# Attention on one core: rounding the next pair's q and k behind the transposed blocks' copies of the same slot

## The reference, cut to what matters

```python
q = rope(xn @ q_w + q_b)            # 16 heads of 64
k = rope(xn @ k_w + k_b)
scores = (q @ k.T) / sqrt(64)
attn = softmax(where(causal, scores, -inf))
ctx = attn @ (xn @ v_w + v_b)
attn_out = ctx @ o_w + o_b + xn
```

## Time and profile before

| | |
|---|---|
| median of 3 runs | 2509.33 us (2506.49 to 2509.35) |
| profiled execution | 2507.55 us, of which the instructions span 2505.6 us |
| TensorE busy | 2063.1 us (82%), weight loads beside it 1363.4 us |
| VectorE busy | 1666.8 us (67%) |
| ACT busy | 1440.3 us (57%) |
| POOL busy | 920.0 us (37%) |
| mean granted TensorE clock | 0.916 |

### The profile page before, as it was taken

One profiled execution on the slowest core, in us unless ns is written; L12 is line 12 of the kernel. 1 busy time (PEld: TensorE's weight loads), 2 busy tenths in 40 slices (PEclk: granted clock), 3 DMA queues, 4 the chain that ended last, 5 costly groups with the idle time before them and its releaser, 6 DMA issues.

```text
span 2505.6 us, 41253 instructions
## 1 busy us (share of the span) xinstructions
PE 2063.1 (82%) x10326; PEld 1363.4 (54%) x10326; DVE 1666.8 (67%) x2947; ACT 1440.3 (57%) x2785; POOL 920.0 (37%) x797
## 2 busy tenths in 40 slices
PE   3749999879675999987966699996996669999698
PEld 1236666547324666655732466664662256666466
DVE  3957676669485666647948666674794766666488
ACT  2517676647542766655744366674674346766366
POOL 1544343223164434313315444341332453434222
PEclk9879999979796999997979799999897979999899
DMA  2000000001000000001100000000110000000011
GB/s 60 0 26 5 9 8 0 1 28 40 10 0 26 10 5 8 0 1 34 34 10 0 26 10 5 8 0 9 30 30 10 13 14 8 9 4 0 11 34 32
DMA packets 36210, 35.48 MB, mean 14 GB/s; under 512 B 3992, under 2 KB 30976, under 8 KB 36096
## 3 DMA queue, kind: packets, MB, share of 16 engines
q1 hardware_dynamic: 36096, 34.14, 4.7%
HBM read 32.03 MB, written 2.10 MB: 14 GB/s over the span
## 4 chain that ended last, share of the span: by engine, by line
PE 59%; DVE 20%; issue 10%; ACT 5%; POOL 4%; DVEq 1%; ACTq 0%; DMA 0%; POOLq 0%; SPq 0%
PE ps L1341 10%; PE ps L1180 7%; PE ps L1181 7%; PE ps L1182 7%; PE ps L1330 6%; DVE state L930 6%; PE ps L1320 4%; PE ps L1321 4%; PE ps L1356 3%; PE ps L1448 2%; PE ps L1208 2%; DVE q_split L993 2%; PE ps L1172 2%; DVE bx L923 2%; DVE ps L1008 1%
## 5 line engine op out<-in xcount | busy, mean ns | idle before, releaser
L707 ACT ACTIVATE probsT<-ps 128x512 f32<-128x512 f32 (+3 forms) x768 | 349.6, 493 | 382.4 <-PE ps L1330 381.7
L695 ACT ACTIVATE probs<-ps,least 128x640 f32<-128x640 f32 (+7 forms) x512 | 380.6, 743 | 65.4 <-DVE least L1003 59.5
L1330 PE MATMUL ps<-ident,probs 128*128 128x128 f32 x2304 | 349.4, 279 | 10.4 <-ACT probsT L707 10.2
L1320 PE MATMUL ps<-k_high,q_split 128*128 128x512 f32 (+3 forms) x768 | 309.2, 403 | 57.8 <-POOL k_low L550 38.6
L1330 PEld LDWEIGHTS ps<-ident,probs 128*128 128x128 f32 x2304 | 262.9, 141 | 128.2 <-issue 91.6
L538 POOL TENSOR_TENSOR roped<-turned 128x512 f32<-128x512 f32 x128 | 192.6, 1506 | 286.1 <-DVE turned L978 274.2
L1341 PE MATMUL ps<-probsT,vals 128*64 128x512 f32 (+3 forms) x1536 | 290.4, 502 | 5.2 <-ACT probsT L707 5.2
L1003 DVE CUSTOM_DVE_ANT_0 ps<-ps,row_masks 128x128 f32<-128x128 f32 (+3 forms) x256 | 127.6, 499 | 235.2 <-PE ps L1321 232.5
L1010 DVE TENSOR_REDUCE least<-ps 128x1 f32<-128x640 f32 (+3 forms) x256 | 262.3, 1025 | 9.1
L1321 PE MATMUL ps<-k_low,q_split 128*128 128x512 f32 (+3 forms) x768 | 259.0, 349 | 0.0
L755 ACT ACTIVATE hid<-ps,cols 128x512 f32<-128x512 f32 x256 | 176.4, 689 | 105.2 <-PE ps L1182 77.1
(11 more groups left out here) (213 smaller groups left out, 4252.2 us busy)
## 6 DMA issues: line engine op xcount, KB each, us to landing
w<-in_w SPq DMA_DIRECT2D x128, 128.0 KB, 2.0
w_pair<-in_w_pairs SPq DMA_DIRECT2D x36, 256.0 KB, 2.7
xin<-in_x SPq DMA_DIRECT2D x5, 512.0 KB, 3.9
out<-acc SPq DMA_DIRECT2D x4, 512.0 KB, 4.1
pos<-in_c_pos SPq DMA_DIRECT2D x1, 512.0 KB, 5.5
v_w<-in_v_w SPq DMA_DIRECT2D x1, 512.0 KB
o_w<-in_o_w SPq DMA_DIRECT2D x1, 512.0 KB
v_b<-in_v_b SPq DMA_DIRECT2D x1, 512.0 KB
```

Source lines behind the costliest of these rows:

```text
L695: act.activation(probs[:, t % 2, 0:width(t)], banks(2 * (t % 2))[:, 0:width(t)], ACT.Exp, bias=least[:, t:t + 1], scale=-1.0, accum_out=ro ...
L707: act.activation(dst, ps[:, T_BANK + g % 2, 0:k1 - k0], ACT.Copy).then_inc(t_taken, 1)
L1320: pe.matmul(o, q, k_high[par][h][:, k0:k1], start=True, stop=False)
L1330: made = pe.transpose(ps[:, T_BANK + g % 2, at - k0:at - k0 + P], probs[:, t % 2, at:at + P], ident[:, :])
```

## The change

In ACT's `step`, the rounding of a slot is issued behind the copies of the transposed block instead of ahead of them. It concerns slots 5, 6, 9 and 10 of the first seven pairs of each batch.

```diff
@@ -720,12 +720,12 @@
                             keep_factors(n - 1, 1, x_at(p, "old", 0, first, last))
                         if t == SPREAD_AT[0]:
                             keep_factors(n, 0, x_at(p, "own", 0, first, last))
-                        if t in HIGH_AT and not last:
-                            high(n + 1, 1 - par, *HIGH_AT[t])
                         if t > 0:
                             keep_turned(n, t - 1)
                         elif not first:
                             keep_turned(n - 1, UNITS_A - 1)
+                        if t in HIGH_AT and not last:
+                            high(n + 1, 1 - par, *HIGH_AT[t])
```

## The result

| | before | after |
|---|---|---|
| median | 2509.34 us (2506.49 to 2509.73, 4 runs) | 2535.23 us (2533.49 to 2538.1, 4 runs) |
| ratio to before | | 1.0106, 95% interval 1.009 to 1.0122 |
| span of the profiled execution | 2505.6 us | 2531.5 us |
| mean granted TensorE clock | 0.916 | 0.916 |

What follows compares the result with a forecast made beforehand. TensorE was busy 82% of the span, with VectorE's full queue leading slots 7 to 10. 24 x 0.95 = 22.8 plus 4 x 0.71 = 2.8 gave 25.6 us more: median 2535.0 us, range 2523 to 2543.

Steps and rivals of the forecast that it cites:

- Slot 5, 0.95 us in 24 pairs: Steady pairs: the moved rounding delays exponential 6 and the scores of unit 8 by 0.95 us, bracket nothing to 1.08.
- Slot 5, 0.71 in four first pairs: First pair of each batch, no ACT idle time in slot 5: exponential at 193.40 against 192.69, 0.71 us later.
- Slots 6, 9 and 10, nothing: Roundings moved in these three slots delay later exponentials, but TensorE wants those later still: cost nothing.
- cover of slot 9: Slot 9: exponential 10's reading ends at 281.98, TensorE wants it at 282.65: 0.67 us of cover.
- cover of slot 6: Slot 6: exponential 7 is ready at 275.32, scores of unit 9 want it at 276.21: 0.89 us of cover.
- Low parts and POOL, nothing: VectorE's low parts of q and POOL's of k wait for their own queues, not ACT's roundings: no cost.
- the booked wait in the first pairs: TensorE's scores of unit 8: booked wait for ACT around 0.6 us or more in 24 pairs, shorter in four first pairs.
- VectorE leads the pair there: Slots 7 to 10: VectorE's full queue, busy 7.77 of 8.00 us, leads the pair, so delayed unit 8 scores delay the rest.
- Rival A: Behind slot 6: an unseen slack swallows the 0.95 us, ACT being idle 43% of the span; 2509 us, chance 0.05.
- Rival B: TensorE's or VectorE's queue gives some back, leaving 0.3 to 0.6 us a pair; 2522 us, chance 0.08.
- Rival C: Slots 9 and 10 are exposed too, up to 0.95 us more a pair; 2562 us, chance 0.04.
- Rival D: Slots 6, 9 and 10: earlier copies free transpose banks, so transposes start sooner; 2499 us at best, chance 0.02.

Runs made afterwards that it cites:

- only_6_9_10: Kernel before with the roundings of slots 6, 9 and 10 put behind the copies, slot 5 in the old order: 2507.04 us, ratio 1.0002.
- low11_after: Kernel before with all four roundings behind the copies and VectorE's second low part of q in slot 11 instead of 8: 2507.65 us.
- double5_ahead: Kernel before with an idle second rounding added in slot 5, ahead of the copy: 2499.81 us.
- double9_ahead: Kernel before with an idle second rounding added in slot 9, both roundings ahead of the copies: 2508.01 us, ratio 0.9999.
- the two halves: Two kernels, each with part of the change against the kernel before: slot 5 alone, ratio 1.0108; slots 6, 9 and 10 alone, ratio 1.0002.
- double9_behind: Kernel before with slot 9's k rounding put behind the copies, together with an idle second rounding of the same size: 2497.62 us.
- low_at_11: Kernel before with VectorE's second low part of q moved from slot 8 to slot 11: 2473.84 us, ratio 0.9864.
- low_at_12: Kernel before with VectorE's second low part of q moved from slot 8 to slot 12: 2485.56 us.

## Why the prediction was right

*Slot 5, 0.95 us in 24 pairs.* Right in place, size and mechanism: the steady pairs went from 40.1 and 40.5 us (they alternate) to 41.0 and 41.5. The bracket of nothing to 1.08 was closed by the row of another rounding, and that row, not the middle of the bracket, was the measured value. *Slot 5, 0.71 in four first pairs:* 0.71 from exponential 5 to exponential 6 in each; up to slot 9 the four batches are 0.64, 0.76, 0.75 and 0.75 longer, 2.9 in all against 2.8. *Slots 6, 9 and 10, nothing:* shown by only_6_9_10, and the cover of slot 9 by spending it. The cover of slot 6 was put too high: 0.89 was worked out, and in the kernel after the scores of unit 9 start only 0.60 behind the reading of exponential 7, because TensorE comes to them 2.80 us after the scores of unit 8 and not 2.97. That cost nothing. *Low parts and POOL, nothing:* TensorE's wait for POOL's low parts of k is 38.7 us after and 38.6 before. The sum, 25.6, stands against 25.9 between the medians and 26.4 in the attention. The 24 steady pairs as measured are 22.5 us longer and the first pairs 2.9, together 25.4; the remaining us of the attention lies in the last pairs, which are 0.2 to 0.3 longer each, a term that the sum put at nothing and that I did not explain. One sign was wrong: the booked wait in the first pairs is 0.69 as in the steady ones, and not shorter.

One reason carried less than the prediction put on it. "VectorE leads the pair there" is true: in the kernel after, TensorE's wait for the values is 1.29 instead of 1.12, so VectorE's queue swallows the 0.17 that TensorE gains. But low11_after shows that the exchange costs 0.86 of the 0.95 once VectorE has slack. The rest of the delay is passed on by the second way, from TensorE through exponential 8 to the scores of unit 10, which the prediction did not name.

That the median fits to 0.3 us is in part luck. The time outside the attention has more than one value (below), up to 5 us a batch apart, and the prediction had no term for it; before and after happen to lie on the same side.

*Rival A.* ACT is busy 57% of the time and has idle time in every pair, but the moved rounding has left an idle stretch for one place that has none. The advice of the Trainium skill (Perfetto Trace Analysis, Identifying the Most-Contended Engine), to improve the engine of the highest occupancy, does not tell the price of an order on a less busy one: 25.9 us here. double5_ahead and double9_ahead are the other side of this: a whole added rounding a pair, at the right place, costs a steady pair nothing. *Rival B* and *Rival C* fell with the two halves, *Rival D* with the unchanged 10.2 us of the earlier trace rows.

## What to carry to other kernels

An instruction on an engine with idle time is free only inside a particular stretch of it; ask of each idle stretch who ends it and what is queued behind, and count a moved instruction at its start-to-start time if it lands between a release and the instruction that someone waits for. A start that always follows its release by the same small latency (0.05 to 0.06 us here) is a critical hand-over even where no wait is booked. In a steady pair of the kernel before six of the sixteen units release TensorE so (units 2, 4, 6, 8, 13 and 15, in all 24 pairs), and only that of unit 6 has an edited slot just ahead of it; what a delay costs at the other five was not tried. Two ways can also be tight at one place, and slack on one of them then gives little back. Compare stages by their own time before reading a small difference of medians as the effect of an edit: in double9_behind the direct cost and a gain elsewhere have opposite signs.

## What was not expected

Several kernels with *more* work or later work in the attention ran faster than before or than foreseen, because the time outside the attention, which no edit touched, has more than one value: 305.3 us a gap, or 299.9 to 300.6. The gap after the first batch, busy time by stretch (columns as in the earlier trace rows), in before, in low_at_11 and in double9_behind:

```profile
493.70:798.90 305.20, 224.35 (x838) 134.53 (x836) 206.02 (x308) 149.92 (x214) 112.14 (x106) 0.84 0.07 21
```

```profile
488.00:788.10 300.10, 218.55 (x838) 130.02 (x836) 205.99 (x308) 149.66 (x214) 112.15 (x106) 0.87 0.07 22
```

```profile
493.00:793.00 300.00, 220.82 (x852) 131.96 (x850) 207.22 (x309) 152.13 (x219) 109.90 (x106) 0.87 0.07 22
```

The first two have the same counts of instructions, and VectorE and ACT the same busy time, but the granted clock is 0.84 in one and 0.87 in the other: TensorE stands at its lower level for 99 us of the gap in before and for 80 in low_at_11. In low_at_12 both kinds of gap stand in one execution: 305.6, 299.9 and 305.5 us, with 99, 80 and 99 us at the lower level. Over the whole span it is 420 us in the execution before and 367 in low_at_11 and double9_behind. To tell whether the edits did this or only their timing, two kernels delay the end of each batch's attention and do nothing else:

```diff
                 keep_turned(b * PAIRS + PAIRS - 1, UNITS_A - 1)
+                act.wait_ge(x_out, X_ALL * b + X_ALL - 1)
+                for i in range(1):                               # delay_2: range(2)
+                    act.activation(xnT_m[HD * i:HD * i + HD, :], xnT[HD * i:HD * i + HD, :], ACT.Copy)
                 keep_factors(b * PAIRS + PAIRS - 1, 1, X_ALL - 2)
```

> The kernel before with one idle ACT copy (64 x 1024, 0.95 us start to start) per batch on the path at the end of the attention: behind the wait for the spread inverses of the last pair, ahead of the copy of the factors. Nothing else differs. Three runs so far had 5 us less a batch outside the attention and a mean granted clock of 0.926 instead of 0.916, though nothing there was edited. Theory P (where the stretches of half clock fall depends on the moment at which the attention ends in relation to something periodic; any small delay can flip it): either 4 x 0.95 = 3.8 us more, 2511 to 2514, or, if it flips, about 3.8 - 15 to 20, 2489 to 2498, with clock 0.926. Theory Q (the edits inside the attention brought it, for instance through a busier ACT or VectorE): 3.8 more and clock 0.915 in every run.

> The same with two idle copies a batch, 1.9 us. Theory P: 7.6 us more, 2515 to 2518, or with a flip 2493 to 2502 and clock 0.926; with delays of 0.95 and 1.9 at least one should flip, since the runs that did differ from before by 2 to 5 us a batch. Theory Q: 2515 to 2518 and clock 0.915.

Both came out faster than before, delay_1 at 0.9966 (0.9955 to 0.9978) and delay_2 at 0.9972 (0.9962 to 0.9981), so Theory Q is out: added idle work of 1 to 2 us a batch made the kernel 8 us faster. Theory P is borne out in the main, though the median of delay_1 lies above its 2489 to 2498 and the clocks go from 0.921 to 0.927 and not straight to 0.926. The executions of one and the same kernel differ too: of the 12 of delay_2 eight lie at 2497.6 to 2500.0 us and four at 2505.9 to 2507.1. The profiled ones are among the slow ones (2505.70 and 2506.59), so the rows of the table do not show the 8 us; their attention sums are 1248.6 and 1249.1 us. In that of delay_1 the first gap is 305.4 us and the second and third are 302.8 and 302.6, so the change of clock can set in midway, and the gap has at least a third value. Shown is that timing alone moves the stretches of low clock; gaps with less of them are up to 5 us shorter here. What decides where they fall stays open, and a kernel that lands on the good side does so by luck. The 15.6 us of low_at_11 in the gaps are of this kind, and so a part of its lead could be lost by the next edit.

The second thing is what VectorE and POOL do to each other when both run two-input operations from SBUF. The low part of q takes 1.22 us in the kernel before and 2.54 in slot 11, beside POOL's low part of k, and the second of these 3.16 instead of 2.37. POOL in low_at_11, in order of time; VectorE's low part stands above, at 281.85:

```profile
280.95 2.37 POOL L550 TENSOR_TENSOR k_low<-roped,k_high 64x1024 fp32r<-64x1024 f32 x1 [0.16 <-POOL k_high L441]
283.47 3.16 POOL L550 TENSOR_TENSOR k_low<-roped,k_high 64x1024 fp32r<-64x1024 f32 x1 [0.16 <-POOL k_low L550]
```

The Trainium skill (GPSIMD Engine Reference, Specifications) names SBUF interfaces shared with VectorE, with contention where a VectorE instruction has two SBUF inputs; this trace agrees. The ends tell more than the durations. POOL's first instruction began first and keeps its 2.37, up to 283.32; VectorE's ends 1.07 later, at 284.39; POOL's second ends 2.24 behind that, at 286.63. Each ends about its own undisturbed time (1.22 and 2.37) after the other's end, less some 0.15, as if the later starter stood still until the earlier one was done. The kernel before has the other order in slot 7, VectorE first by 0.05 (all engines, in order of time):

```profile
270.06 1.28 POOL L538 TENSOR_TENSOR roped<-turned 128x512 f32<-128x512 f32 x1 [3.71 <-DVE turned L978]
...
275.08 1.22 DVE L993 SCALAR_TENSOR_TENSOR q_split<-roped,q_split 64x1024 fp32r<-64x1024 f32 x1
275.13 2.31 POOL L538 TENSOR_TENSOR roped<-turned 128x512 f32<-128x512 f32 x1 [3.79 <-DVE turned L978]
```

There VectorE keeps its 1.22 and only POOL pays, 2.31 instead of 1.28. So it is the one that starts later that waits, and slot 11, where POOL is already at work, is a dearer place for the low part than VectorE's idle time there suggests. No run here varies the order of the two by itself.
